# VectorE adds the gathered rows of the next group behind the first key of a step's second quad

## What is computed

```python
h = relu(layernorm(x))
hid = relu(concat(h[src], edge_attr) @ W1 + b1)          # one row per edge
agg = segment_sum(hid @ W2 + b2, dst)
g = relu(concat(h, agg) @ U1 + c1)
x = x + (g @ U2 + c2)
h = relu(layernorm(x))
x = x + segment_sum(h[src] * edge_weight[:, None], dst)
```

## Time and profile before

| | before |
|---|---|
| time, median of 3 runs | 3135.02 us (3133.75 to 3136.86) |
| the profiled execution's own time | 3122.63 us |
| its span | 3120.8 us |
| busy: PE, DVE, POOL, ACT | 2232.2, 1629.2, 1560.8, 849.5 us |
| share of the span: PE, DVE, POOL, ACT | 72%, 52%, 50%, 27% |
| mean granted TensorE clock | 0.81 of full speed |

### The profile page before, as it was taken

One profiled execution on the slowest core, in us unless ns is written; L12 is line 12 of the kernel. 1 busy time (PEld: TensorE's weight loads), 2 busy tenths in 40 slices (PEclk: granted clock), 3 DMA queues, 4 the chain that ended last, 5 costly groups with the idle time before them and its releaser, 6 DMA issues.

```text
span 3120.8 us, 49909 instructions
## 1 busy us (share of the span) xinstructions
PE 2232.2 (72%) x18336; PEld 1691.8 (54%) x18336; DVE 1629.2 (52%) x4964; ACT 849.5 (27%) x1500; POOL 1560.8 (50%) x1635
## 2 busy tenths in 40 slices
PE   4475755666666677677777777777777777777799
PEld 4354544444444455555555555555555655665577
DVE  4445755555555555555554555545555455554455
ACT  4122433222222222222222222223222322222221
POOL 4635255555555545555555455555555544554400
PEclk9867877777777777777777877888888889888899
DMA  4123444433543454355435543553555356525688
GB/s 89 34 91 133 167 135 154 156 129 121 178 137 118 131 186 149 93 167 166 138 108 164 169 132 119 162 170 114 166 166 154 102 160 181 176 78 155 177 275 289
DMA packets 376799, 459.49 MB, mean 147 GB/s; under 512 B 78474, under 2 KB 298890, under 8 KB 372968
## 3 DMA queue, kind: packets, MB, share of 16 engines
q1 hardware_dynamic: 317914, 401.54, 39.4%
q0 software_dynamic: 51712, 53.06, 7.8%
q10 hardware_dynamic: 6926, 1.63, 0.2%
HBM read 281.50 MB, written 174.54 MB: 146 GB/s over the span
## 4 chain that ended last, share of the span: by engine, by line
PE 51%; issue 16%; another core or an unknown queue 15%; DVE 13%; DMA 2%; ACT 1%; SPq 1%; DVEq 0%; ACTq 0%
PE pair L1303 17%; PE pair L1318 9%; PE pair L1342 7%; PE pair L1243 5%; DVE bld L1818 4%; DVE bld L1828 4%; PE pair L1290 3%; PE pair L1349 2%; PE pair L1236 2%; PE pair L1446 1%; DVE rings L1772 1%; PE pair L1376 1%; DMA late_piece<-adjacency 1%; DVE bld L1821 1%
## 5 line engine op out<-in xcount | busy, mean ns | idle before, releaser
L835 POOL DMA_INDIRECT rows<-table,idx x1464 | 1402.6, 958 | 1245.6 <-DVE rings L1772 851.5
L1009 ACT COPY stage<-pair 128x600 f32<-128x600 f32 x808 | 527.8, 666 | 1760.0 <-remote 767.0
L1818 DVE TENSOR_SCALAR bld<-iota_key,key 128x300 bf16<-128x300 f16 x1616 | 536.8, 332 | 798.8 <-remote 509.7
L1303 PE MATMUL pair<-bld 128*128 128x300 bf16 x4848 | 839.1, 328 | 91.8 <-issue 54.1
L1303 PEld LDWEIGHTS pair<-bld 128*128 128x128 bf16 x4848 | 566.1, 122 | 322.3 <-issue 160.4
L1318 PE MATMUL pair<-stage,h 125*64 125x96 f32 x4230 | 380.0, 310 | 191.2 <-issue 188.8
L1828 DVE TENSOR_TENSOR bld<-bld,part 128x512 bf16<-128x512 bf16 x1212 | 490.7, 405 | 0.0
L1318 PEld LDWEIGHTS pair<-stage,h 125*64 125x64 f32 x4230 | 301.6, 179 | 241.5 <-issue 240.8
L1243 PE MATMUL pair<-w1b,rings 128*128 128x128 f32 x1584 | 264.4, 321 | 164.5 <-DVE rings L1772 160.8
L1243 PEld LDWEIGHTS pair<-w1b,rings 128*128 128x128 f32 x1584 | 244.5, 233 | 185.3 <-DVE rings L1772 176.5
L1342 PE MATMUL pair<-late_piece,h 125*64 125x384 f32 (+1 forms) x1040 | 266.5, 642 | 92.9 <-issue 76.8
(11 more groups left out here) (178 smaller groups left out, 1439.1 us busy)
## 6 DMA issues: line engine op xcount, KB each, us to landing
late_piece<-adjacency SPq DMA_DIRECT2D x232, 480.0 KB
rings<-in_edge_attr_dram SPq DMA_DIRECT2D x202, 256.0 KB
adjacency<-stage SPq DMA_DIRECT2D x14, 2160.0 KB
tail<-stage SPq DMA_DIRECT2D x101, 240.0 KB
stage<-tail SPq DMA_DIRECT2D x50, 480.0 KB, 5.9
rows<-table,idx POOLq DMA_INDIRECT x1464
adjacency<-stage SPq DMA_DIRECT2D x10, 1920.0 KB
adjacency<-stage SPq DMA_DIRECT2D x10, 1680.0 KB
```

What stands on the lines that cost most here:

```text
L835: pool.indirect_dma_start(out=to[:, t, :], out_offset=None, in_=table, in_offset=bass.IndirectOffsetOnAxis(ap=idx[:, g, t:t + 1], axis=0), ...
L1009: act.copy(tiles[:, g % STAGE, :, 2 * j * WT:2 * (j + 1) * WT].rearrange("p h (o w) -> p o h w", w=WT), build_pair[i % 2][:, :, 0:KEYS].re ...
L1303: last = pe.matmul(build_pair[i // 2 % 2][:, t % 2, 0:KEYS], hot_w[q % 2][k][:, :, u], hot_key[q % 2][:, u, :], start=(k == 0), stop=(k == ...
L1818: return dve.tensor_scalar(hot_key[q % 2][:, u, :], iota_key[:, :], key[:, g, t + u:t + u + 1], None, ALU.is_equal)
```

## The change

`make_quad` gets an optional argument: the group whose rows are to be added. In the second quad of step s (quad 2s + 3), `add_fast(s + 1)` is issued right behind the first key, and no longer at the head of step s + 1 behind `add_sums(s)`. This holds for groups from `RAW` = 4 on; groups 0 to 3 stay as they were.

```diff
--- before.py
+++ after.py
@@ -1811,7 +1811,7 @@
                 dve.tensor_reduce(hot_sum[:, g % TWO, :], hot[:, g % TWO, :, :].rearrange("p t w -> p w t"), AX_X,
                                   ALU.add).then_inc(hot_summed, 1)
 
-            def make_quad(q):
+            def make_quad(q, take=None):
                 g, t = q // 2, q % 2 * 4
 
                 def keys_of(u):
@@ -1824,6 +1824,8 @@
                 for k in range(PARTS):
                     keys_of(k)
                     if k == 0:
+                        if take is not None:
+                            add_fast(take)
                         dve.wait_ge(eq_made, q + 1)
                     dve.tensor_tensor(hot_w[q % 2][k], hot_eq[q % 2], over(part[k][:, g, t:t + 4], P), ALU.mult)
                 keys_of(PARTS).then_inc(quad_made, 1)
@@ -1860,8 +1862,9 @@
                 for s in range(GROUPS):
                     if 1 <= s <= GROUPS:
                         add_sums(s - 1)
+                    if s < RAW:
+                        add_fast(s)
                     if s < GROUPS:
-                        add_fast(s)
                         make_hot(s)
                     if s + 1 < RAW:
                         centre_raw(s + 1)
@@ -1873,7 +1876,7 @@
                     keep_late(s - 1, 1 if many == 3 else 0, many)
                     for q in (2 * s + 2, 2 * s + 3):
                         if q < 2 * GROUPS:
-                            make_quad(q)
+                            make_quad(q, s + 1 if q % 2 == 1 and s + 1 >= RAW else None)
                         if q % 2 == 0 and s + 1 < RAW:
                             variance_raw(s + 1)
                             normalise_raw(s + 1)
```

## The result

The changed kernel takes 3416.16 us (median of 4 runs, 3398.85 to 3419.03) against 3134.39 us for the kernel before (4 runs): a ratio of 1.089, 95% interval 1.0851 to 1.093. It is 9% slower where 3.4% faster was forecast. The profiled execution took 3415.93 us.

What follows compares the result with a forecast made beforehand. No engine is full; gathers waiting for `add_fast` were the largest wait (851.5 of 3120.8 us). Terms -100 - 13 - 10 + 15 = -108 gave 3014.6, with 12.4 for the runs' median 3027 us; range 2930 to 3150.

Steps and rivals of the forecast that it cites:

- The loop: Middle stretch: gather's end releases DVE, DVE's work releases the next gather; 9.7 + 1.79 + 2.28 + 0.96 = 14.7 us a group.
- Term 1: Middle stretch, 800 to 2400 us: 111 gaps before gathers shrink by 0.9 us each, -100 us; -158 if all kept.
- The slower rival: Tiles fall behind the gather's last release, once copies come later than 8.6 us in; +84 or 3219 us; chance 0.18.
- The late stretch: 2400 to 2980 us, 37 gathers: shifting the next gather forward gives -10 us, between -73 and +26.
- signs of being wrong: Second quad's key over 12 us into the gather, copies behind its end, TensorE's wait grown over 0.7, or `add_fast` awaiting `gathered`.
- Term 2: Early stretch, 200 to 800 us: about an eighth of the -110 us bound is won, -13; upwards +43.
- Term 4: Second quad's products beside the gather's first indirect DMAs: 0.1 us for some 150 gathers, +15; bounds 0 and +77.
- the contention rival: Contention of products with indirect DMAs is usual, not rare: +77 in place of +15, 3089 us; chance 0.05.
- `add_sums` later by 0.69: Nothing in the early stretch, counted inside the middle stretch's term; 77 us on TensorE if direct products didn't cover it.
- What was read as given: Anything DVE awaits from TensorE and not seen early in a gather is seen about 1.8 us after it; cause unexplained.

Runs made afterwards that it cites:

- e1: The changed kernel with `add_fast` behind the last key of the second quad instead of the first, still ahead of `add_sums`; 3219.55 us, ratio 1.025.
- e2: The changed kernel with its gather made to wait in addition for the additions of sums, so it starts about where it did before; 3207.87 us, ratio 1.0213.
- e4: The changed kernel with its gather held in addition until tiles 0 to 3 of the step are built; 3218.83 us, ratio 1.0247.
- j1: Sums, then rows, both behind the second quad's first key, against the kernel before on a fifth chip, one with the hold; 3049.96 us, ratio 0.9874.

## Why the prediction was wrong

- **The loop.** Right as read for the kernel before: gather, 1.8 us, VectorE, gather. In the changed kernel `add_fast` does follow the first key by 0.21 us (2.28 before), so the gather starts sooner after its releaser. But the second quad's key is no longer what is seen 1.8 us behind the gather's end. ScalarE's copy is, and the key comes 4.01 us behind that.
- **Term 1 (-100), the step that failed.** "Between keeping all of 1.42 and falling to the late stretch's gap I take 0.9 us a group, nearer to the first because the middle stretch has its tiles 4 to 7 still ahead of the gather's end by this shift." Measured +172 us. I worked out that the copies of tiles 0 to 3 would come 6.4 us into the gather and treated that as room left up to 8.6, because a late group has copies at 5.8 and 8.6. That was a misreading: the pairs of those two copies had ended 3.07 and 3.83 us into the gather and were themselves held for 2.76 and 4.79 us, and the usual copy of that stretch was at 3.3. The shift was smaller than I took, not larger. In the group shown the late products did start 2.8 us deeper, but they took 1.51 us at a granted clock of 1.00 where they had taken 2.83 at 0.51, so the tiles start only 1.2 us deeper. That was enough: of the pairs that end 4.5 to 6 us in, 95 of 135 were held already in the trace before (the table). Once tiles 0 to 3 are seen only behind the gather, tiles 4 to 7 can't lie ahead of its end at all.
- **The slower rival.** This is what happened, with its mechanism as written and both numbers wrong. It decides far ahead of 8.6 us: most pairs are held from 4.5 us on, and in the changed kernel earlier (the table). And its price isn't the late stretch's gap: 6.2 us a gap and not 5.23, as 4.01 us of copying and building stand behind the release, 1.46 of them from the lower clock, which has no term in the prediction. It had 0.18; its +84 was less than half. The late stretch, for which I took -10 and at worst +26, lost 109 in the same way. Two of the signs of being wrong that the prediction names are what the trace shows: the second quad's key over 12 us into the gather (15.56 in the group above) and copies behind its end. e1, e2 and e4 show that the place of the gather decides: each puts it later or moves it less, and each is 190 to 210 us below the changed kernel's 3416 us (another set of runs; as ratios 1.021 to 1.025 against 1.089). j1 keeps the tiles' place and wins 1.3%.
- **Term 2 (-13).** Measured +5. Only 7 of the 34 gathers followed the one before at once; most of the others kept a gap near 3 us. For these 7 "what is won in one gap is lost in the other" is right, and the second of a pair loses some more than I read from the earlier trace rows. That the stretch came out near the forecast is in part luck.
- **Term 4 (+15) and the contention rival.** The mean of an indirect DMA is 951 ns against 958 before: over 1464 of them -10 us where +15 was forecast. Contention is there but small: in the kernel before, the 535 indirect DMAs beside one of the quad's products took 974 ns on average and the 929 others 949, and 90 and 12 of them took over 1 us. The change moves products to the gather's first DMAs, but fewer stand beside a product in all, 451. So the Trainium skill's statement on shared SBUF interfaces (GPSIMD Engine Reference, section 1, Specifications) agrees with this trace in that it occurs, by 25 ns a DMA and not by the 430 of the bound.
- **`add_sums` later by 0.69.** Called included; in e2, where the gather is back in its place and the sums are late, the kernel is 2.1% slower than before, 66 us. This has also an added wait in it, so the 66 us hold both costs.
- **What was read as given.** "That TensorE's results are seen so late ... I take it as it is." It is not a property of this program alone. Where it is absent the kernel takes 2234 us, GpSimd is the bound, and the change gives 1.0019.

Not settled: what holds the semaphores, from which point on, and why on some chips and not on others. It is not shown whether DMAs, the semaphores' own way or the recording of the trace does it. The late products and the clock were not varied on their own, so what the low clock costs is read from the traces and not tested.

## What to carry to other kernels

Before an engine's long activity (here a gather) is started earlier, don't only ask how much shorter the loop behind it gets. Look where in that activity each result of the other engines ends, by the end of the instruction and not by the time at which somebody acts on it, and count what crosses into the part where results are seen late. Here the work that crossed cost more than the loop had won, and it was then done at the lower clock. What helped was to move the sums and the rows together (j1). And measure on a second chip before a tuning step is believed: the two changes of order here are worth 9% and -1.3% on one and 0.2% and 0.9% on another.

## What the runs showed of the hardware

- One kernel took 3134, 3142 and 3093 us in three sets of runs (the last two on two chips) and 2234, 2237 and 2233 us on three other chips, each time within 0.6% over its runs. The instructions' own times on GpSimd and VectorE are nearly the same: an indirect DMA 958 and 966 ns, `add_fast` 688 ns in both. What differs is the time between TensorE's end and the sight of its semaphores: 0.04 us there throughout, here a median of 2.4 to 6.6 us for pairs that end 4.5 to 6 us into a gather, as much as 7.9 us in a single gather (j1) and 16.3 (the changed kernel) where two gathers follow each other at once. The granted clock is 0.81 on the one and 0.94 on the other, where TensorE idles less.
- The traces of chips with the hold also record fewer semaphore updates: for the kernel before, 683 of the 808 updates of `pair_built` against 803 on the third chip, and 18,933 updates by DMAs against 45,728. I know no reason; it fits a semaphore path that is congested there, which is argued and not shown, and against it stands that the changed kernel, which loses more by the hold, has 767 of the 808.
- An indirect DMA for 128 rows of 256 bytes takes GpSimd 0.95 to 0.97 us on average, and there are 0.30 us between two, on every chip that was profiled. For the 183 groups from 19 on that is 183 x 8 x 1.25 = 1830 us of the 2234 on the chips without the hold, and with half of them left out from group 22 on the kernel takes 2062.
- Behind 5.92 idle us TensorE built four tiles in 3.16 us at a granted clock of 0.50; at 1.00 the same four take 1.70 us. In the changed kernel this is the usual case for tiles 4 to 7 (66 of 109 groups), in the kernel before it is rare (5).
